# Cross-attention and a 4-bit FFN on one core: the second layernorm's halves transposed by DMA, and all FFN groups of a batch one step later

## The reference

```python
n1   = layernorm(x)                                   # over the last axis, 1024
q, k, v = Wq @ n1, Wk @ ctx, Wv @ ctx                 # C = 128 channels
attention = softmax(q^T k / sqrt(C))                  # [1024, 256] per batch
x1   = x + Wskip @ n1 + v @ attention^T
w    = (int4(qweight) - round(zeros / scales)) * scales   # [1024, 1024]
out  = x1 + layernorm(x1) @ w + bias
```

## Time and profile before

| | |
|---|---|
| time, median of 3 runs (lowest to highest) | 616.7 us (616.62 to 617.56) |
| the profiled execution: its own time | 616.67 us |
| its span, first to last instruction | 614.8 us |
| granted TensorE clock, mean | 0.989 |
| busy: PE, PEld, DVE, ACT, POOL | 96%, 68%, 77%, 67%, 76% |
| chain that ended last, by engine | PE 91%, DVE 5%, ACT 2%, issue 1%, DMA 1% |
| DMA queue q1 (issued by SyncE), share of 16 engines | 19.7% |

### The profile page before, as it was taken

One profiled execution on the slowest core, in us unless ns is written; L12 is line 12 of the kernel. 1 busy time (PEld: TensorE's weight loads), 2 busy tenths in 40 slices (PEclk: granted clock), 3 DMA queues, 4 the chain that ended last, 5 costly groups with the idle time before them and its releaser, 6 DMA issues.

```text
span 614.8 us, 10932 instructions
## 1 busy us (share of the span) xinstructions
PE 588.1 (96%) x3348; PEld 416.1 (68%) x3348; DVE 476.5 (77%) x1027; ACT 409.4 (67%) x976; POOL 468.7 (76%) x520
## 2 busy tenths in 40 slices
PE   2868999999999999999999999999999999999996
PEld 2755777667777766777776677777677777667763
DVE  6787877878887777888778788878777877887762
ACT  4874677666668766666876666686666677666650
POOL 2453788777879877777977787897778789777866
PEclk9977999999999999999999999999999999999999
DMA  8011012222111222211222211122221112221002
GB/s 315 3 43 43 27 53 79 77 77 73 40 53 66 77 77 77 70 41 47 73 77 77 77 65 46 43 77 77 77 77 54 57 43 77 77 77 68 19 19 102
DMA packets 20178, 41.38 MB, mean 67 GB/s; under 512 B 2496, under 2 KB 7104, under 8 KB 20160
## 3 DMA queue, kind: packets, MB, share of 16 engines
q1 hardware_dynamic: 19584, 41.03, 19.7%
q10 hardware_dynamic: 576, 0.14, 0.1%
HBM read 24.39 MB, written 16.78 MB: 67 GB/s over the span
## 4 chain that ended last, share of the span: by engine, by line
PE 91%; DVE 5%; ACT 2%; issue 1%; DMA 1%; POOLq 0%; POOL 0%; ACTq 0%
PE ps_y L676 36%; PE ps_e L610 17%; PE ps_o L644 14%; PE ps_t L625 9%; PE ps_o L637 7%; PE ps_t L657 5%; PE ps_kv L688 2%; PE ps_kv L686 2%; DMA sb_x<-in_x_dram 1%; DVE sb_nib L457 1%; ACT sb_prob L288 1%; DVE sb_pt_lo L408 1%; DVE sb_neg_max L398 0%; ACT sb_pt_hi L297 0%; DVE sb_zp L499 0%
## 5 line engine op out<-in xcount | busy, mean ns | idle before, releaser
L288 ACT ACTIVATE sb_prob<-ps_e,sb_neg_max 128x256 f32<-128x256 f32 x256 | 118.7, 470 | 128.9 <-DVE sb_neg_max L398 128.8
L676 PE MATMUL ps_y<-sb_wf,sb_xnt_hi 128*128 128x512 f16 x512 | 196.1, 383 | 0.9 <-DVE sb_xnt_lo L448 0.9
L676 PE MATMUL ps_y<-sb_wf,sb_xnt_lo 128*128 128x512 f16 x512 | 194.0, 379 | 0.0
L214 POOL TENSOR_SCALAR sb_prob<-sb_prob,sb_rsum 128x256 f32<-128x256 f32 x256 | 117.7, 477 | 27.5 <-DVE sb_rsum L403 27.5
L408 DVE TENSOR_TENSOR sb_pt_lo<-ps_t,sb_pt_hi 128x512 fp32r<-128x512 f32 x128 | 88.3, 691 | 34.6 <-ACT sb_pt_hi L297 30.4
L398 DVE TENSOR_REDUCE sb_neg_max<-ps_e 128x2 f32<-128x512 f32 x128 | 87.7, 686 | 34.8 <-PE ps_e L610 34.8
L610 PE MATMUL ps_e<-sb_kv_hi,sb_xc_hi 128*128 128x256 f32 x256 | 91.6, 358 | 7.7 <-DVE sb_kv_lo L535 4.0
L297 ACT ACTIVATE sb_pt_hi<-ps_t 128x512 fp32r<-128x512 f32 x128 | 76.3, 598 | 33.9 <-PE ps_t L625 33.9
L676 PEld LDWEIGHTS ps_y<-sb_wf,sb_xnt_hi 128*128 128x128 f16 x512 | 49.7, 97 | 59.2 <-issue 17.6
L223 POOL TENSOR_TENSOR sb_rstd<-sb_ve,sb_neg_half 128x1 f32<-128x1 f32 x32 | 17.5, 548 | 92.3 <-DVE sb_ve L443 92.3
L250 POOL TENSOR_TENSOR sb_xc_lo<-sb_xc,sb_xc_hi 128x1024 fp32r<-128x1024 f32 x32 | 76.5, 2390 | 9.2 <-ACT sb_xc_hi L343 7.5
(11 more groups left out here) (85 smaller groups left out, 1162.9 us busy)
## 6 DMA issues: line engine op xcount, KB each, us to landing
sb_x<-in_x_dram SPq DMA_DIRECT2D x32, 512.0 KB, 3.3
out_dram<-sb_o SPq DMA_DIRECT2D x64, 256.0 KB, 2.1
sb_ctx<-in_ctx_dram SPq DMA_DIRECT2D x32, 128.0 KB, 2.5
sb_q<-in_L_ffn_qweight_dram SPq DMA_DIRECT2D x4, 512.0 KB, 6.4
sb_scale_row<-in_L_ffn_scales_dram SPq DMA_DIRECT2D x1, 512.0 KB, 8.7
sb_bias_row<-in_L_ffn_bias_dram SPq DMA_DIRECT2D x1, 512.0 KB, 9.5
sb_wk<-in_L_xattn_Wk_dram SPq DMA_DIRECT2D x1, 64.0 KB, 3.4
sb_wq<-in_L_xattn_Wq_dram SPq DMA_DIRECT2D x1, 64.0 KB, 3.3
```

Source lines behind the costliest of these rows:

```text
L214: last = pool.tensor_scalar(prob[:, j, t, :], prob[:, j, t, :], rsum[:, j, t:t + 1], 1.0, ALU.mult, ALU.mult)
L288: done = act.activation(prob[:, j, t, :], ps_e[j % 2][:, t, :], ACT.Exp, bias=neg_max[:, j, t:t + 1], accum_out=esum[:, j, t:t + 1])
L676: last = pe.matmul(ps_y[h][:, :], xnt_p[s][:, kt, :], wf[:, kt, h * HALF:(h + 1) * HALF], start=kt == 0 and s == 0, stop=kt == KT - 1 and ...
```

## The change

`xn` is no longer transposed on TensorE. ScalarE and VectorE split the untransposed `xn` in two fp16 halves, `xn_hi` and `xn_lo` (`split_xn`, `split_xn_lo`), and SyncE issues two DMA transposes, SBUF to SBUF, 128 x 1024 fp16 each, into `xnt_hi` and `xnt_lo`, which now have two buffers. The eight FFN groups of batch `b - 2` all run in step `b`: each group now stands where the one two places further on stood, and the last two, (1, 2) and (1, 3), stand at the places shown below. `scale_product(., 1)` moves from the end of a step to behind the first row maximum of the next. The number of steps is the same.

```diff
-        xnt_hi, xnt_lo = (sb(n, [P, KT, P], F16) for n in ("xnt_hi", "xnt_lo"))
+        xn_hi, xn_lo = (sb(n, [P, KT, P], F16) for n in ("xn_hi", "xn_lo"))
+        xnt_hi, xnt_lo = (sb(n, [P, 2, KT, P], F16) for n in ("xnt_hi", "xnt_lo"))
...
@@ SyncE, step, between the stores and the loads
+                if ran(p):
+                    sp.wait_ge(xnhi_done, p + 1)
+                    if ran(p, 2):
+                        sp.wait_ge(y_done[1], p - 1)
+                    sp.dma_start_transpose(xnt_hi[:, 1 - par, :, :], xn_hi[:, :, :].rearrange(
+                        "c k r -> c (k r)")).then_inc(xnt_loaded[1 - par], 16)
+                    sp.wait_ge(xnlo_done, p + 1)
+                    sp.dma_start_transpose(xnt_lo[:, 1 - par, :, :], xn_lo[:, :, :].rearrange(
+                        "c k r -> c (k r)")).then_inc(xnt_loaded[1 - par], 16)
...
@@ ScalarE
-            def xn_hi(p, h):
-                act.wait_ge(xnt_done[h], p + 1)
-                if h == 0 and ran(p, 1):
-                    act.wait_ge(y_done[1], p)
-                act.activation(xnt_hi[:, 4 * h:4 * h + 4, :], ps_t[h][:, :].rearrange("p (k r) -> p k r", r=P),
-                               ACT.Copy).then_inc(xnthi_done[h], 1)
+            def split_xn(p, par):
+
+                act.wait_ge(xn_done, p + 1)
+                if ran(p, 1):
+                    act.wait_ge(xnt_loaded[1 - par], arrived(p - 1, 1 - par, 32))
+                act.activation(xn_hi[:, :, :].rearrange("c (t e) r -> c t e r", e=2),
+                               xn[:, :].rearrange("c (t r e) -> c t e r", e=2, r=P),
+                               ACT.Copy).then_inc(xnhi_done, 1)
...
                 if ran(b):
                     probs_hi(b, 1)
+                if ran(p):
+                    split_xn(p, 1 - par)
...
-                if ran(p):
-                    xn_hi(p, 0)
-                    xn_hi(p, 1)
...
@@ VectorE
-            def xn_lo(p, h):
-                dve.wait_ge(xnthi_done[h], p + 1)
-                dve.tensor_tensor(xnt_lo[:, 4 * h:4 * h + 4, :], ps_t[h][:, :].rearrange("p (k r) -> p k r", r=P),
-                                  xnt_hi[:, 4 * h:4 * h + 4, :], ALU.subtract).then_inc(xntlo_done[h], 1)
+            def split_xn_lo(p, par):
+
+                dve.wait_ge(xnhi_done, p + 1)
+                if ran(p, 1):
+                    dve.wait_ge(xnt_loaded[1 - par], arrived(p - 1, 1 - par, 32))
+                dve.tensor_tensor(xn_lo[:, :, :].rearrange("c (t e) r -> c t e r", e=2),
+                                  xn[:, :].rearrange("c (t r e) -> c t e r", e=2, r=P),
+                                  xn_hi[:, :, :].rearrange("c (t e) r -> c t e r", e=2),
+                                  ALU.subtract).then_inc(xnlo_done, 1)
...
                 if ran(b):
                     row_max(b, 0)
+                if ran(b - 3):
+                    scale_product(b - 3, 1)
...
                     probs_lo(b, 1)
+                if ran(p):
+                    split_xn_lo(p, 1 - par)
...
                 if ran(q):
                     scale_product(q, 0)
-                    scale_product(q, 1)
...
@@ TensorE
-            def transpose_xn(b, p, h):
...
-                    ffn(q, 0, 2)
+                    ffn(q, par, 0, 0)
...
                     transpose_probs(b, 3)
+                if ran(q):
+                    ffn(q, par, 1, 2)
                 if ran(n):
                     keys_values(n, 1 - par)
-                if ran(p):
-                    transpose_xn(b, p, 0)
                 if ran(b):
                     skip(b, par, 1)
-                if ran(p):
-                    transpose_xn(b, p, 1)
+                if ran(q):
+                    ffn(q, par, 1, 3)
                 if ran(b):
                     attend(b, par, 1)
-                if ran(p):
-                    ffn(p, 0, 0)
-                    ffn(p, 0, 1)
```

More of the change, by code:

```diff
@@ L127, in xattn_ffn_program @@
         nb2_done, xn_done = sem("nb2"), sem("xn")
-        xnt_done, xnthi_done, xntlo_done = sems("xnt", HALVES), sems("xnthi", HALVES), sems("xntlo", HALVES)
+        xnhi_done, xnlo_done, xnt_loaded = sem("xnhi"), sem("xnlo"), sems("xnt_loaded", 2)
         zpt_done, addbias_done, rest_done = sem("zpt"), sem("addbias"), sem("rest")
@@ L168, in step @@
             def step(b, par):
-                c = b - 3
+                c, p = b - 3, b - 1
                 if ran(c):
@@ L182, in step @@
                     sp.dma_start(x_sb[:, par, :], x[b + 2, :, :]).then_inc(x_loaded[par], 16)
-            run_steps(sp, step)
+            for b in range(-1, B + 3):
+                step(b, b % 2)
             for par in range(2):
@@ L320, in step @@
                     if ran(p, 1):
-                        act.wait_ge(xnt_done[1], p)
+                        act.wait_ge(xnlo_done, p)
                     act.activation(xn[:, :], x1[:, 1 - par, :], ACT.Identity, bias=nb2[:, :],
@@ L525, in finish @@
                     stats2(b, par, 0)
-                if ran(p):
-                    xn_lo(p, 0)
-                    xn_lo(p, 1)
                 if ran(n):
@@ L620, in transpose_probs @@
                     pe.wait_ge(ptlo_done[j + 2], b)
-                if j < 2 and ran(b, 2):
-                    pe.wait_ge(xntlo_done[j], b - 1)
                 for m in range(MT):
@@ L646, in attend, with ffn @@
                 last.then_inc(attn_done[h], 1)
-            def transpose_xn(b, p, h):
-                pe.wait_ge(xn_done, p + 1)
-                if ran(b):
-                    pe.wait_ge(ptlo_done[2 + h], b + 1)
-                else:
-                    pe.wait_ge(xntlo_done[h], p)
-                for k in range(4):
-                    t, e = (4 * h + k) // 2, k % 2
-                    last = pe.transpose(ps_t[h][:, k * P:(k + 1) * P],
-                                        xn[:, 2 * P * t + e:2 * P * (t + 1):2], ident[:, :])
-                last.then_inc(xnt_done[h], 1)
-            def ffn(c, h, g):
+            def ffn(c, cpar, h, g):
                 if g == 0:
                     if h == 0:
-                        pe.wait_ge(xntlo_done[0], c + 1)
+                        pe.wait_ge(xnt_loaded[cpar], arrived(c, cpar, 32))
                     if ran(c, 1):
                         pe.wait_ge(prod_done[h], c)
-                if g == 2 and h == 0:
-                    pe.wait_ge(xntlo_done[1], c + 1)
                 if isinstance(c, int) and c == 0 and h == 0:
@@ L675, in ffn @@
                     for s in range(2):
-                        last = pe.matmul(ps_y[h][:, :], xnt_p[s][:, kt, :], wf[:, kt, h * HALF:(h + 1) * HALF],
+                        last = pe.matmul(ps_y[h][:, :], xnt_p[s][:, cpar, kt, :], wf[:, kt, h * HALF:(h + 1) * HALF],
                                          start=kt == 0 and s == 0, stop=kt == KT - 1 and s == 1)
@@ L704, in step @@
                 if ran(q):
-                    ffn(q, 0, 3)
+                    ffn(q, par, 0, 1)
                 if isinstance(b, int) and b == 0:
@@ L710, in step @@
                 if ran(q):
-                    ffn(q, 1, 0)
+                    ffn(q, par, 0, 2)
                 if ran(b):
@@ L716, in step @@
                 if ran(q):
-                    ffn(q, 1, 1)
+                    ffn(q, par, 0, 3)
                 if ran(b):
@@ L720, in step @@
                 if ran(q):
-                    ffn(q, 1, 2)
+                    ffn(q, par, 1, 0)
                 if ran(b):
@@ L725, in step @@
                 if ran(q):
-                    ffn(q, 1, 3)
+                    ffn(q, par, 1, 1)
                 if ran(b):
```

## The result

| | before | changed |
|---|---|---|
| time, median (lowest to highest) | 616.66 us (615.67 to 617.56, 4 runs) | 647.07 us (646.04 to 648.81, 4 runs) |
| ratio to before, 95% interval | | 1.0496 (1.0467 to 1.0526) |
| span of the profiled execution | 614.8 us | 645.9 us |
| granted TensorE clock, mean | 0.989 | 0.988 |
| a steady step (mean of 22) | 18.01 us | 18.90 us |

The kernel became 5% slower; 649 us had been forecast. The mean clock is the same in both, and it is 1.00 over the steady steps (151 to 566 us) of both, so it has no part in what a step costs.

A forecast was written before the change was run, and what follows sets the result against it. TensorE was taken as the bound (busy 588.1 of 614.8 us), with two chains through VectorE closely under it. 614.8 + 29 x 1.05 + 2 = 647.3 of span, plus 1.9: 649 us; 8 in 10 for 612 to 672.

The forecast's parts named there:

- The two meetings: VectorE stands for GpSimd: split_xn_lo until addbias ends, ending 321.45 not 319.6; wsk_lo until rest ends, 326.2.
- The size of a step: Between second residual adds on VectorE: 19.06 us instead of 18.01, 1.05 longer.
- The ends: Outside the 29 steady steps: start-up -2, last full step +1.5, drain +2.5, together +2 us.
- The drain: After the last steps: batch 30's eight FFN groups must cover layernorm, halves and transfers; +2.5 us, between 0 and +6.
- The last full step: Eight FFN groups instead of six (+1.76), no transposes (-0.94), stall at skip(1) (about +0.9): +1.5 us.
- The transfers: Two 256 KB DMA transposes a step, taken at 4 us each, so nothing on the path.
- The upper bound: DMA transpose in 256-byte pieces, 64 per queue at 0.099 us a packet: 6.3 us and a landing.
- The lock does not bite: Faster rival: split_xn_lo costs only its 1.1 us, wsk_lo meets nothing; step 17.5, 604 us; chance 0.17.
- Only the second meeting: Slower rival: split_xn_lo gets through, but wsk_lo waits for rest; step 18.5, 633 us; chance 0.10.
- the cover in front of the scores: Two FFN groups (2 x 0.88 us) between attention product and first scores move away; step 17.5 if all else is hidden.
- the likeliest range: Case with both or the first meeting, chance 0.60: 636 to 662 us, steps 18.6 to 19.4, ends -1 to +5.
- Slow transposes: Rival: each DMA transpose needs 8 us, the low half lands 4.8 late, step 23.6, about 780 us; chance 0.10.

The follow-up runs named there:

- x_wait: Changed kernel, with GpSimd's addbias of a batch also waiting until split_xn_lo of that batch is done: 605.36 us.
- x_bn: Changed kernel, with split_xn_lo's subtraction replaced by two one-input bn_stats on VectorE, low halves left as zeros: 635.01 us.
- x_rest: Changed kernel, with GpSimd's rest also waiting for kv_lo of the next batch: 641.01 us.
- x_cover: x_wait with the last FFN group, (1, 3), moved behind attend(b, 1), in front of the next scores: 603.29 us.
- x_early: x_wait with wsk_hi and wsk_lo moved early, behind split_xn and split_xn_lo, and addbias waiting for wsk_lo: 608.54 us.
- x_best: x_early with the last FFN group, (1, 3), moved behind the attention product again: 587.68 us.
- x_half: Changed kernel, with GpSimd's addbias in two instructions of 512 columns and no wait added: 610.38 us.

## Why the prediction was right, and where its sum was not

**The two meetings.** They stand in the trace as forecast, nearly to the digit. Measured from the last residual add of the step before: split_xn begins at 9.32 (forecast 9.32) and takes 1.15; addbias ends at 12.40 (12.41), split_xn_lo at 13.48 (13.51), rest at 18.05 (18.26), and the next residual add begins at 18.85 in this step, 18.90 in the mean (19.06). x_wait, x_bn and x_rest show that each of the two is a cause and not merely there.

The Trainium skill (SBUF — State Buffer, section "SBUF: two separate sides") gives the rule for these two engines, an exclusive lock held for a whole instruction, against a VectorE instruction with two SBUF inputs. The trace agrees: 1.08 and 0.15 us behind the ends of GpSimd's instructions, against bn_stats with one SBUF input that keeps its 0.69 beside addbias. One SBUF input alone is no safeguard, though: the nibble shift reads a single SBUF tensor, began while xc_lo ran on GpSimd (45.06 to 47.56) and took 2.83 us, where the shift before it took 0.68.

**The size of a step** was 0.16 us too long. The term is the one that starts xc_lo when split_xn_lo is through and gives it 2.39 more: it began at 315.15, while split_xn_lo was still running, and ended at 317.85, 2.23 after it. (The recorded sum is also a little short: 326.2 + 0.15 + 0.39 + 0.33 is 327.07, not 327.0.) Over 29 steps, with a first step that was 0.3 shorter than before rather than longer, this makes +24.4 and not +30.4.

**The ends** were off the other way. The start-up was put at -2 and came to +1.87: the step that failed is "two groups of transposes and an FFN pair leave TensorE, while split_xn_lo lands in VectorE's chain: -2". There the chain runs on VectorE, where TensorE's saving counts for little. It reads (changed kernel, 20 to 57 us):

```profile
42.65 0.04 DVE sb_xn_lo L463
42.69 3.35 issue
46.04 2.00 DVE sb_zps_row L523 x2
```

Another 0.96 was lost before batch 0's second residual add (32.39 against 31.43); that may be scatter, since x_wait and x_cover, the same as the changed kernel up to there, have 31.61 and 33.18. The drain came to +3.36 and not +2.5, inside the bounds given. Half of it is a term that the prediction lacked. The last sixteen FFN matmuls, before and after (chain of waits):

```profile
603.16 3.64 PE ps_y L676 x16
...
632.54 5.33 PE ps_y L676 x16
```

They come behind the wait for xnt_lo, in which TensorE stood for 3.53 us, and from 632.9 to 636.8 us its granted clock was 0.57, near the lower of its two levels, 1.2 GHz. That is 1.69 us. The last full step came out at +1.43 against +1.5, but its terms (1.76 - 0.94 + 0.9) add up to 1.7. So the 649 owes its closeness in part to two misses of opposite sign, -6 in the steps and +4.7 at the ends, beside the mechanism.

**The transfers** were hidden, as forecast, and landed in 3.1 us, not 4, between the two bounds. The upper bound was built from 0.099 us a packet. Each transpose makes (87168 - 19584) / 64 = 1056 packets, about as assumed, but they add only (645.9 x 0.322 - 614.8 x 0.197) x 16 / 67584 = 0.021 us each. A packet's time taken from large packets was five times too much for small ones. By the Trainium skill (VectorE: DVE Perf Modes, section "The three transpose paths") a DMA transpose of 128 x 128 takes 1309 ns; eight in a row would be an estimated 10.5 us. The measured 3.1 decides: the blocks of one large transpose do not cost that one after another.

**The rivals.** "The lock does not bite" was priced at 604 us and a step of 17.5. x_wait, where the long meeting is taken away, has 605.4 and 17.52. "Only the second meeting" was priced at 633 and 18.5; x_bn has 635.0 and 18.58. The case without the second meeting was given a step of 18.75; x_rest has 18.69. The prediction's two limits, 17.5 without the cover in front of the scores and 16.7 with TensorE alone, are met by x_early and x_best, 17.46 and 16.76; one of the two FFN groups was cover enough. Two of its figures do not follow from their terms, and neither bore on the outcome: the lower end of the likeliest range, with a step of 18.6 and ends of -1, is 633 and not 636, and two transposes of 8 us in a row from 318.4 land 6.4 us behind 328, not 4.8. Slow transposes were not seen.

## What to carry to other kernels

Before you put a VectorE instruction with two SBUF inputs into a schedule, look up which GpSimd instruction runs at that moment: a 1.2 us subtraction became one of 3 us here, and the two meetings cost 1.4 us of a step of 18.9, some 40 us of 647. Look at every meeting of the step: without one of the two the kernel gained 6 or 12 us, with both made short 37 to 42. Where GpSimd has slack, as here, it can wait for VectorE (605 us); its instruction cut in two did nearly as well without a wait (610 us). A kernel in which GpSimd has no slack was not tried. And where a saving on the bounding engine brings nothing, expect several chains just under it: undo them one at a time and together, since here either alone was worth 0 to 0.06 us a step and both 0.76.

## What was not expected of the hardware

- A VectorE instruction that stood still has its own time to go behind GpSimd's end, less 0.15 to 0.18 us: 1.07 to 1.08 us of 1.23 for 1024 elements, 0.15 of 0.33 for 128. GpSimd stands in the same way: its second half of addbias in x_half, and xc_lo, which took 2.70 where 2.39 is usual.
- After 3.53 us without work in the drain, TensorE ran at a granted clock of 0.57 for some 4 us.
- The engine that stands gets in at the next instruction boundary even if the other has its next instruction ready: in x_half the pair of halves took 3.52 us and not 2.6.
- A DMA transpose of 256 KB occupies SyncE for 1.24 us at its issue, the load of x for 0.33, and lands after 3.1; a second one in the same queue did not move that beyond 3.3.
